# Rearranging the opening of a fused cross-attention and expert kernel: range sums, exponential table, step 0's exponentials and value banks

## The chip, the cores and the metric

The kernel runs on one core of a Trainium2 chip. The metric is the device time of one execution in microseconds (us), as the median of several runs. Engines are called PE (matmuls), PEld (its weight loads), DVE (vector), ACT (scalar), POOL (GpSimd) and SP (which issues most DMAs). PSUM, the memory that matmuls write into, has eight banks, 0 to 7, each of 128 partitions by 512 fp32.

## The reference, cut to what matters

```python
# x, ctx: [4, 256, 128]; 16 heads of 64; 64 experts, 8 taken per token
xn, ln = layer_norm(ctx), layer_norm(layernorm(x))
q = ln @ Wq
k, v = split(concatenate([xn, ln], axis=1) @ Wkv)   # 512 keys and values per batch, INNER = 1024
attn = softmax(q @ k.T * scale + mask)
x = x + layer_norm((attn @ v) @ Wout)
h = layernorm(x)
x = x + shared_expert(h) + routed_experts(h)
```

## The kernel before, in words

Every engine has its own instruction stream, written out by hand, and the engines meet through semaphores. Products that need fp32 accuracy are split in a high and a low part: a product is three matmuls (high by high, high by low, low by high: lines 761 to 763 in `three`), and every result that is used again is split by ACT (high part) and DVE (low part, which needs the high one).

The program has three stages.

**Prelude.** Weights and tokens are loaded. ACT makes the high parts of the weights (`wv_hi`, `wk_hi`, `wq_hi`), POOL the low parts. DVE computes the moments of the tokens of batches 0 and 1 (`token_moments(0)`, `spread_of(0)`, `normalise_half(0)`), then of batches 2 and 3. ACT takes the roots (`root`), normalises the context tokens (`normalise_context`), and evacuates the transposed tokens (`evac_tokens`) to `kvT`, which DVE's `split_tokens` splits in `kv_hi` and `kv_lo`. For batches 2 and 3 POOL makes `kv_lo`.

Values are kept in fp16 pairs, so they need a scale that keeps them in range. ACT sums the squares of the value weights and of the gains. One matmul with a matrix of ones (L827) spreads the two sums over all partitions, into bank 0 (`OUT_BANK`). DVE's `value_range` (L1165 to L1183) copies them out (L1169, which lifts `s_range` to 2) and computes the scale, whose last instruction lifts `s_range` to 3. It is the last thing in DVE's prelude.

**Opening.** One list, `OPENING`, gives all engines their order: 32 value chunks v0 to v31, and between them the transposes of batches 2 and 3 (t2, t3), keys and queries of the first steps (k0, q0, k1), and step 0's scores (s0, s1), biases (b0, b2) and exponentials (x0 to x3). A value chunk is three matmuls of 512 columns on PE, ACT's scaled copy (L587) and DVE's low part (L1244); its bank is free when that is done. Chunks 0 to 13 go round banks 0, 5, 3 and 4, chunks 14 to 31 round banks 0, 5 and 6. Banks 2, 3 and 4 hold scores from s0 on, bank 1 keys, bank 7 queries. An item "s" is two masked score tiles on DVE (L1202), after PE has made their scores. PE waits for `s_range` 2 before the first item, and for all 32 low parts after the last one.

**Steps.** 32 steps, each one pair of heads of one batch: scores, softmax, split, transposition, attention, projection. PE's loop starts with `clear_out()`, `keys(2)` and `queries(1)` and then `scores(1, 0)`. After the steps come the experts.

The program inserts a load of ScalarE's function table where a function isn't in the table loaded last. `Sqrt` is used in the prelude, `Exp` first in item x0.

Of the kernel before, what the change touches and what calls it, by code (L numbers as in the profile page):

```python
# [29 lines left out]
ACT = mybir.ActivationFunctionType  # L30
# [12 lines left out]
def xattn_moe(nc, x, ctx_in, mask, g_x, b_x, g_l, b_l, wq, wkv, wout, g_o, b_o,  # L43
# [13 lines left out]
    TILES = 2 * QT  # L57
# [4 lines left out]
    with stack:  # L62
        def sem(name):
            return stack.enter_context(nc.semaphore(name))
# [94 lines left out]
        ps = stack.enter_context(nc.psum_tensor("ps", [P, 8, 512], F32))  # L159
        OUT_BANK, K_BANK, SCORE_BANK, TURN_BANK, AV_BANK, Q_BANK = 0, 1, 2, 5, 6, 7  # L160
# [10 lines left out]
        def at_hi(b):  # L171
            return (b + B // 2) % B
# [18 lines left out]

        def v_bank(n):

            return (0, 5, 3, 4)[n % 4] if n < 14 else (0, 5, 6)[n % 3]

        def v_before(n):

            return max((m for m in range(n) if v_bank(m) == v_bank(n)), default=None)
# [3 lines left out]


        CHUNKS = 2 * B * KT
        between = {1: ["t2"], 3: ["t3"], 9: ["k0"], 10: ["q0"], 12: ["k1"], 14: ["s0"], 15: ["b0"], 16: ["x0", "x1"], 17: ["s1"],
                   18: ["b2"], 20: ["x2"], 22: ["x3"]}
        OPENING = [item for n in range(CHUNKS) for item in [f"v{n}"] + between.get(n, [])]
        OPENING = [(item.rstrip("0123456789"), int(item.lstrip("vtkqsxb"))) for item in OPENING]

# [11 lines left out]
        s_squares, s_range = sem("s_squares"), sem("s_range")  # L221
# [4 lines left out]
        s_table = sem("s_table")  # L226
# [12 lines left out]
        s_score, s_masked, s_exp = sem("s_score"), sem("s_masked"), sem("s_exp")  # L239
# [254 lines left out]
        def _(act):  # L494
# [4 lines left out]
            def root(half):  # L499

                act.wait_ge(s_var, half + 1)
                act.activation(rs[:, half * NT:(half + 1) * NT], tmp[:, 0, half * NT:(half + 1) * NT], ACT.Sqrt)\
                    .then_inc(s_std, 1)

            def normalise_context(b):

                if b % 2 == 0:
                    act.wait_ge(s_shift, b // 2 + 1)
                for q in range(QT):
                    j = b // 2 * NT + 4 + b % 2 * QT + q  # L510
                    ins = act.activation(tok[:, b, q, :], tok[:, b, q, :], ACT.Identity,
                                         bias=shift[:, j:j + 1], scale=rs[:, j:j + 1])
                    ins.then_inc(s_tokc, 1)

            def evac_tokens(b):

                act.wait_ge(s_kvtp, b + 1)
                for part in range(2):
                    act.activation(kvT[:, b, part * S:(part + 1) * S],
                                   ps[:, AV_BANK + b % 2, part * S:(part + 1) * S], ACT.Identity,  # L520
                                   bias=cols[:, 2 * part + 1:2 * part + 2],
                                   scale=cols[:, 2 * part:2 * part + 1]).then_inc(s_kvT, 1)
# [16 lines left out]
            evac_tokens(0)  # L539
            root(1)  # L540
            evac_tokens(1)
            normalise_context(2)
            normalise_context(3)
            act.wait_ge(s_wq, 16)
# [212 lines left out]
        def _(pe):  # L757
            def three(o, a_hi, a_lo, b_hi, b_lo, start=True, stop=True):

                skip = not (start and stop)  # L760
                pe.matmul(o, a_hi, b_hi, start=start, stop=False, skip_group_check=skip)  # L761
                pe.matmul(o, a_hi, b_lo, start=False, stop=False, skip_group_check=skip)  # L762
                return pe.matmul(o, a_lo, b_hi, start=False, stop=stop, skip_group_check=skip)  # L763
# [4 lines left out]
            def transpose_tokens(b):  # L768

                pe.wait_ge(s_tok, b + 1)  # L770
                pe.wait_ge(s_tokc, QT * (b + 1))
                if b >= 2:
                    pe.wait_ge(s_kvT, 2 * (b - 1))
                for j in range(KT):
                    mm = pe.transpose(ps[:, AV_BANK + b % 2, j * P:(j + 1) * P], tok[:, b, j, :],
                                      ident[:, :])
                mm.then_inc(s_kvtp, 1)
# [46 lines left out]
                            mm.then_inc(s_score, 1)  # L824

            pe.wait_ge(s_squares, 2)
            pe.matmul(ps[:, OUT_BANK, 0:2], ones[:, :], range_v[:, 0:2], start=True, stop=True).then_inc(s_range, 1)  # L827
            pe.wait_ge(s_wvlo, 1)
            pe.wait_ge(s_range, 2)
            for what, n in OPENING:  # L830
                if what == "v":
                    b, j, half = n // (2 * KT), n // 2 % KT, n % 2
                    if n % (2 * KT) == 0:
                        pe.wait_ge(s_kvlo, b + 1)
                    if v_before(n) is not None:
                        pe.wait_ge(s_vlo, v_before(n) + 1)
                    cut = slice(half * 512, (half + 1) * 512)
                    three(ps[:, v_bank(n), :], kv_hi[:, at_hi(b), j * P:(j + 1) * P],
                          kv_lo[:, b, j * P:(j + 1) * P], wv_hi[:, cut], wv_lo[:, cut]).then_inc(s_v, 1)
                elif what == "t":  # L840
                    transpose_tokens(n)
                elif what == "k":
                    keys(n)
                elif what == "q":
                    queries(n)
                elif what == "s":
                    if n == 0:
                        pe.wait_ge(s_klo, 1)
                        pe.wait_ge(s_qlo, 1)
                        pe.wait_ge(s_vlo, 11)  # L850
                    else:
                        pe.wait_ge(s_vlo, 12)
                    scores(0, n)
# [228 lines left out]
        def _(dve):  # L1082
            count = [0]

            def chain(ins):

                ins.then_inc(s_dve, 1)
                count[0] += 1
# [52 lines left out]
            def normalise_half(half):  # L1141
                at = half * NT
                inverse_std(NT, (s_std, half + 1), at)

                dve.scalar_tensor_tensor(out=shift[:, at + 4:at + NT], in0=mv[:, at + 4:at + NT, 0], scalar=-1.0,
                                         in1=rs[:, at + 4:at + NT], op0=ALU.mult, op1=ALU.mult)\
                   .then_inc(s_shift, 1)
                for b in (2 * half, 2 * half + 1):
                    for q in range(QT):
                        j = at + b % 2 * QT + q  # L1150
                        ins = normalise(tok[:, b, QT + q, :], x_in[:, QT * b + q, :], j)
                        if q == 0:
                            chain(ins)
                    ins.then_inc(s_tok, 1)

            def split_tokens(b):
                dve.wait_ge(s_kvT, 2 * (b + 1))
                dve.tensor_copy(kv_hi[:, at_hi(b), :], kvT[:, b, :]).then_inc(s_kvhi, 1)
                if b >= B // 2:
                    return  # L1160
                dve.wait_ge(s_kvhi, b + 1)
                dve.tensor_tensor(kv_lo[:, b, :], kvT[:, b, :], kv_hi[:, at_hi(b), :].bitcast(F32), ALU.subtract)\
                   .then_inc(s_kvlo, 1)

            def value_range():  # L1165

                bits = range_v[:, :].bitcast(I32)
                dve.wait_ge(s_range, 1)
                dve.tensor_copy(range_v[:, 2:4], ps[:, OUT_BANK, 0:2]).then_inc(s_range, 1)  # L1169
                dve.wait_ge(s_range, 2)  # L1170
                chain(dve.scalar_tensor_tensor(out=range_v[:, 4:5], in0=range_v[:, 2:3], scalar=2.0 * P,
                                               in1=range_v[:, 3:4], op0=ALU.mult, op1=ALU.mult))
                chained()
                chain(dve.tensor_scalar(bits[:, 5:6], bits[:, 4:5], 23, None, ALU.logical_shift_right))
                chained()
                chain(dve.tensor_scalar(bits[:, 5:6], bits[:, 5:6], 1, None, ALU.add))
                chained()
                chain(dve.tensor_scalar(bits[:, 5:6], bits[:, 5:6], 1, None, ALU.logical_shift_right))
                chained()
                chain(dve.tensor_scalar(bits[:, 6:7], bits[:, 5:6], -1, 205, ALU.mult, ALU.add))  # L1180
                chain(dve.tensor_scalar(bits[:, 7:8], bits[:, 5:6], 49, None, ALU.add))
                chained()
                dve.tensor_scalar(bits[:, 6:8], bits[:, 6:8], 23, None, ALU.logical_shift_left).then_inc(s_range, 1)  # L1183
# [5 lines left out]
            token_moments(1)  # L1189
            spread_of(1)  # L1190
            split_tokens(0)
            normalise_half(1)
            split_tokens(1)
            value_range()

            def mask_scores(i, t):

# [246 lines left out]
```

## Time and profile before

| what | us |
|---|---|
| median of 3 runs | 400.32 |
| lowest, highest | 398.47, 401.39 |
| the profiled execution | 398.68 |
| its span | 396.9 |
| PE busy | 350.5 (88%) |
| DVE busy | 310.2 (78%) |
| ACT busy | 288.6 (73%) |
| POOL busy | 234.5 (59%) |

The span is the time from the first to the last instruction that the profiler recorded; 1.8 us of the execution's time lie around it. The profiled execution is 1.6 us below the median of the three runs.

### The profile page before, as it was taken

Reading aid. Unit: us, or ns where it says so; the run is one execution under the profiler, and the core shown is the slowest. Engines: PE = TensorE matmul, PEld = TensorE weight load, DVE = VectorE, ACT = ScalarE, POOL = GpSimd, SP = SyncE. Lnnn points to the kernel's source line nnn. Section 1 sums busy time; section 2 is a strip of 40 time slices with the busy share of each in tenths; the row PEclk is TensorE's granted clock in tenths of the full one; section 3 lists DMA queues with packets and bytes.
Section 4 is the critical chain, followed back from the end, with each engine's and each line's share of the span. In section 5 each row is a group of like instructions: output and inputs, shape, how many; then the busy total and the mean of one; then the engine's idle time right before and its main releaser. Section 6 shows DMA issues by size and latency. Waiting matters only on the chain.

```text
span 396.9 us, 7568 instructions
## 1 busy us (share of the span) xinstructions
PE 350.5 (88%) x2381; PEld 237.9 (60%) x2381; DVE 310.2 (78%) x753; ACT 288.6 (73%) x639; POOL 234.5 (59%) x291
## 2 busy tenths in 40 slices
PE   0259797899999999999999989977899898999995
PEld 0248464566666666666666656755576675677773
DVE  2889676787877877778977877858799888888884
ACT  3469675876867768687799799956387887766662
POOL 5227220978798888887789989899188870000000
PEclk9999969999999999999999999999899999999998
DMA  7500040598979898998788986840000000000000
GB/s 243 147 1 1 2 79 0 106 176 124 183 132 176 132 177 139 168 147 155 125 175 128 158 134 114 127 80 2 2 0 1 2 1 0 2 26 1 2 0 26
DMA packets 117959, 33.65 MB, mean 85 GB/s; under 512 B 107808, under 2 KB 117536, under 8 KB 117920
## 3 DMA queue, kind: packets, MB, share of 16 engines
q1 hardware_dynamic: 117488, 31.60, 45.2%
q10 hardware_dynamic: 432, 1.57, 1.2%
q8 instruction: 19, 0.31, 0.3%
q14 instruction: 20, 0.16, 0.1%
HBM read 8.26 MB, written 0.52 MB: 22 GB/s over the span
## 4 chain that ended last, share of the span: by engine, by line
PE 62%; DVE 14%; issue 7%; ACT 7%; DMA 5%; POOL 4%; SPq 0%; DVEq 0%; ACTq 0%; POOLq 0%
PE ps L821 10%; PE ps L865 8%; PE ps L761 8%; PE ps L762 6%; PE ps L763 6%; PE ps L894 4%; PE ps L906 3%; PE ps L879 3%; PE ps L981 3%; PE ps L1001 3%; PE ps L1003 3%; PE ps L1002 3%; DMA pT<-p 2%; DMA tok<-in_ctx 2%; DVE v L1244 2%
## 5 line engine op out<-in xcount | busy, mean ns | idle before, releaser
L393 POOL TENSOR_TENSOR p<-prob,p 128x512 f16<-128x512 f32 x93 | 108.1, 1163 | 7.5
L1202 DVE CUSTOM_DVE_ANT_0 sc<-ps,mask_add 128x512 f32<-128x512 f32 x128 | 83.3, 688 | 32.9 <-PE ps L821 31.3
L555 ACT ACTIVATE prob<-sc,p_bias 128x512 f32<-128x512 f32 x128 | 91.5, 716 | 3.4 <-POOL p L393 1.4
L391 POOL CAST p<-prob 128x512 f16<-128x512 f32 x93 | 56.7, 610 | 46.7 <-ACT prob L555 33.4
L709 ACT ACTIVATE h<-ps 128x512 f32<-128x512 f32 (+1 forms) x66 | 39.3, 595 | 20.8 <-PE ps L763 20.4
L1376 DVE TENSOR_TENSOR h<-h,ps 128x512 f32<-128x512 f32 x64 | 43.8, 684 | 12.9 <-PE ps L981 12.6
L1383 DVE TENSOR_TENSOR h_lo<-h,h_hi 128x512 fp32r<-128x512 f32 (+1 forms) x66 | 49.4, 748 | 3.1 <-ACT h_hi L722 3.0
L722 ACT ACTIVATE h_hi<-h 128x512 fp32r<-128x512 f32 (+1 forms) x66 | 41.4, 627 | 14.2 <-DVE h L1376 13.5
L865 PE MATMUL ps<-pT,v 128*64 128x256 f16 x768 | 48.0, 275 | 0.0
L563 ACT ACTIVATE p_bias<-neg_max,ln_range 128x2 f32<-128x2 f32 x64 | 18.6, 290 | 37.9 <-DVE neg_max L1202 37.8
L865 PEld LDWEIGHTS ps<-pT,v 128*64 128x64 f16 x768 | 39.5, 110 | 5.2 <-issue 3.7
L761 PE MATMUL ps<-xf_hi,wu_hi 128*128 128x512 f32 x64 | 37.0, 578 | 0.0
L821 PE MATMUL ps<-k_hi,q_hi 64*128 64x512 f32 x128 | 32.0, 495 | 4.1 <-DVE neg_max L1202 2.5
L1225 DVE TENSOR_TENSOR pT<-ps,pT 128x512 f16<-128x512 f32 x35 | 23.6, 678 | 7.2 <-ACT pT L571 7.0
L1244 DVE SCALAR_TENSOR_TENSOR v<-ps,range_v,v 128x512 f16<-128x512 f32 x32 | 23.1, 749 | 7.8 <-ACT v L587 7.5
L981 PE MATMUL ps<-cwT,sel 128*128 128x512 f16 x64 | 25.2, 397 | 2.0 <-DVE h L1376 2.0
L1001 PE MATMUL ps<-h_hi,wd_hi 128*128 128x512 f32 x64 | 26.2, 409 | 0.2 <-DVE h_lo L1383 0.2
L587 ACT ACTIVATE v<-ps,range_v 128x512 f16<-128x512 f32 x32 | 21.2, 686 | 6.8 <-PE ps L763 4.0
L763 PE MATMUL ps<-xf_hi,wu_lo 128*128 128x512 f32 x64 | 25.5, 399 | 0.0
L762 PE MATMUL ps<-xf_lo,wu_hi 128*128 128x512 f32 x64 | 25.5, 399 | 0.0
L821 PE MATMUL ps<-k_lo,q_hi 64*128 64x512 f32 x128 | 25.5, 392 | 0.0
L821 PE MATMUL ps<-k_hi,q_lo 64*128 64x512 f32 x128 | 25.5, 391 | 0.0
(187 smaller groups left out, 758.9 us busy)
## 6 DMA issues: line engine op xcount, KB each, us to landing
wup_s<-in_L_ffn_W_up SPq DMA_DIRECT2D x8, 256.0 KB, 3.5
wdn_s<-in_L_ffn_W_down SPq DMA_DIRECT2D x8, 256.0 KB, 3.7
pT<-p SPq DMA_TRANSPOSE x93, 3.2
wkv_s<-in_L_xattn_Wkv ACTq DMA_DIRECT2D x2, 512.0 KB, 5.9
x_in<-in_x SPq DMA_DIRECT2D x2, 256.0 KB, 7.2
tok<-in_ctx SPq DMA_DIRECT2D x4, 128.0 KB, 8.0
wq_s<-in_L_xattn_Wq ACTq DMA_DIRECT2D x1, 512.0 KB, 8.3
wo_s<-in_L_xattn_Wout SPq DMA_DIRECT2D x1, 512.0 KB, 5.1
```

Source lines behind the costliest of these rows:

```text
L391: pool.tensor_copy(p16[:, t, 0, :], prob[:, t, :]).then_inc(s_phi, 1)
L393: pool.tensor_tensor(p16[:, t, 1, :], prob[:, t, :], p16[:, t, 0, :], ALU.subtract).then_inc(s_plo, 1)
L555: act.activation(prob[:, t, :], sc[:, t, :], ACT.Exp, bias=p_bias[:, t:t + 1], scale=-1.0, accum_out=p_sum[:, i % 2, t:t + 1]).then_inc(s_ ...
L722: act.activation(h_hi[0:rows_of(g), g % SPLIT_RING, :], h[0:rows_of(g), g % H_RING, :], ACT.Copy)\
L761: pe.matmul(o, a_hi, b_hi, start=start, stop=False, skip_group_check=skip)
L762: pe.matmul(o, a_hi, b_lo, start=False, stop=False, skip_group_check=skip)
L763: return pe.matmul(o, a_lo, b_hi, start=False, stop=stop, skip_group_check=skip)
L821: mm = pe.matmul(ps[:, score_bank(i, 2 * qt + head), :], a[rows, i // 2 % 2, at:at + P], c[rows, i % 2, :], start=(n == 0), stop=(n == 2), ...
L865: mm = pe.matmul(ps[cut, AV_BANK, 0:S], v16[:, b * KT + j, v, pair * P + head * DH:pair * P + (head + 1) * DH], pT[:, i % 2, head, p * KT ...
L1202: return dve.tensor_tensor_reduce(sc[:, t, :], ps[:, score_bank(i, t), :], mask_add[:, step(i)[2], :], -SCALE, -LEAST, ALU.add, ALU.min, n ...
L1376: dve.tensor_tensor(h[:, g % H_RING, :], h[:, g % H_RING, :], ps[:, CW_BANK + weighed(g) % 2, :], ALU.mult).then_inc(s_h, 1)
L1383: dve.tensor_tensor(h_lo[rows, g % SPLIT_RING, :], h[rows, g % H_RING, :], h_hi[rows, g % SPLIT_RING, :].bitcast(F32), ALU.subtract).then_ ...
```

## The change

- The range sums go to bank 2 (`SCORE_BANK`), and PE's wait for `s_range` 2 moves from before v0 to before s0.
- DVE's `value_range()` moves from the end of the prelude to behind `split_tokens(0)`, ahead of `normalise_half(1)`.
- ACT gets one more instruction, an `Exp` of one column, behind `evac_tokens(1)`; it brings the table load with it.
- x1 moves from directly behind x0 (chunk 16) to behind v18, and b2 from behind v18 to behind v19.
- From v20 on, chunks go round banks 5, 2, 6, 3, 0, 4. Those that use banks 2, 3 or 4 first wait until all four masked tiles of step 0 are made (`s_masked` 4).

```diff
         def v_bank(n):
-            return (0, 5, 3, 4)[n % 4] if n < 14 else (0, 5, 6)[n % 3]
+            return (0, 5, 3, 4)[n % 4] if n < 14 else (0, 5, 6)[n % 3] if n < 20 else (5, 2, 6, 3, 0, 4)[n % 6]
...
-        between = {1: ["t2"], 3: ["t3"], 9: ["k0"], 10: ["q0"], 12: ["k1"], 14: ["s0"], 15: ["b0"], 16: ["x0", "x1"], 17: ["s1"],
-                   18: ["b2"], 20: ["x2"], 22: ["x3"]}
+        between = {1: ["t2"], 3: ["t3"], 9: ["k0"], 10: ["q0"], 12: ["k1"], 14: ["s0"], 15: ["b0"], 16: ["x0"], 17: ["s1"],
+                   18: ["x1"], 19: ["b2"], 20: ["x2"], 22: ["x3"]}
...
             evac_tokens(1)
+            act.activation(tmp[:, 1, 0:1], ident[:, 0:1], ACT.Exp).then_inc(s_table, 1)
             normalise_context(2)
...
             pe.wait_ge(s_squares, 2)
-            pe.matmul(ps[:, OUT_BANK, 0:2], ones[:, :], range_v[:, 0:2], start=True, stop=True).then_inc(s_range, 1)
+            pe.matmul(ps[:, SCORE_BANK, 0:2], ones[:, :], range_v[:, 0:2], start=True, stop=True).then_inc(s_range, 1)
             pe.wait_ge(s_wvlo, 1)
-            pe.wait_ge(s_range, 2)
             for what, n in OPENING:
                 if what == "v":
...
+                    if n >= 20 and v_bank(n) in (2, 3, 4):
+                        pe.wait_ge(s_masked, TILES)
...
                     if n == 0:
+                        pe.wait_ge(s_range, 2)
                         pe.wait_ge(s_klo, 1)
...
                 dve.wait_ge(s_range, 1)
-                dve.tensor_copy(range_v[:, 2:4], ps[:, OUT_BANK, 0:2]).then_inc(s_range, 1)
+                dve.tensor_copy(range_v[:, 2:4], ps[:, SCORE_BANK, 0:2]).then_inc(s_range, 1)
...
             split_tokens(0)
+            value_range()
             normalise_half(1)
             split_tokens(1)
-            value_range()
```

## Rows read from the trace of the kernel before

**Rows 1.** Windows: stretch, length, busy PE, PEld, DVE, ACT, POOL, clock, DMA share, GB/s.

```profile
24.30:40.30 16.00, 15.98 (x62) 12.65 (x62) 14.25 (x25) 12.86 (x22) 10.15 (x5) 1.00 0.00 1
40.30:51.10 10.80, 7.15 (x31) 4.10 (x30) 7.59 (x16) 7.04 (x14) 3.47 (x4) 0.96 0.08 16
51.10:64.10 13.00, 11.46 (x33) 7.71 (x33) 9.57 (x13) 9.63 (x17) 1.77 (x2) 0.77 0.26 49
...
80.00:260.00 180.00, 177.00 (x1545) 116.43 (x1544) 143.47 (x397) 145.21 (x373) 150.86 (x183) 1.00 0.87 149
```

**Rows 2.** Timeline, prelude: start, duration, engine, line, operation [idle time before it].

```profile
13.58 2.34 POOL L370 TENSOR_TENSOR wk_lo<-wkv_s,wk_hi 128x1024 fp32r<-128x1024 f32 x1 [4.73 <-ACT wk_hi L533]
13.63 2.30 DVE L1145 SCALAR_TENSOR_TENSOR shift<-mv,rs 128x4 f32<-128x4 f32 x1
...
20.25 0.69 DVE L1162 TENSOR_TENSOR kv_lo<-kvT,kv_hi 128x512 fp32r<-128x512 f32 x1
...
21.89 0.16 DVE L1145 SCALAR_TENSOR_TENSOR shift<-mv,rs 128x4 f32<-128x4 f32 x1
...
22.09 1.65 ACT L511 ACTIVATE tok<-tok,shift,rs 128x128 f32<-128x128 f32 x4 [1.05 <-DVE shift L1145]
...
23.64 1.05 ACT L545 ACTIVATE wq_hi<-wq_s 128x1024 fp32r<-128x1024 f32 x1
...
24.32 0.77 PE L761 MATMUL ps<-wv_hi,kv_hi 128*128 128x512 f32 x1 [5.17 <-DVE range_v L1169]
...
24.77 2.37 POOL L372 TENSOR_TENSOR wq_lo<-wq_s,wq_hi 128x1024 fp32r<-128x1024 f32 x1 [8.85 <-ACT wq_hi L545]
...
25.26 1.90 DVE L1183 TENSOR_SCALAR range_v<-range_v 128x2 int32<-128x2 int32 x1
...
27.20 1.26 ACT L587 ACTIVATE v<-ps,range_v 128x512 f16<-128x512 f32 x2 [2.51 <-DVE range_v L1183]
```

**Rows 3.** Timeline of the opening, DVE alone (v4 to v9, v13 and v14).

```profile
32.49 4.04 DVE L1244 SCALAR_TENSOR_TENSOR v<-ps,range_v,v 128x512 f16<-128x512 f32 x6
...
40.52 1.43 DVE L1244 SCALAR_TENSOR_TENSOR v<-ps,range_v,v 128x512 f16<-128x512 f32 x2
```

**Rows 4.** Timeline of the opening around step 0's scores.

```profile
44.12 0.30 ACT L563 ACTIVATE p_bias<-neg_max,ln_range 128x2 f32<-128x2 f32 x1 [1.17 <-DVE neg_max L1202]
...
45.00 1.28 ACT L555 ACT_TABLE_LOAD   x1
...
46.30 0.72 ACT L555 ACTIVATE prob<-sc,p_bias 128x512 f32<-128x512 f32 x1
...
47.73 1.24 ACT L587 ACTIVATE v<-ps,range_v 128x512 f16<-128x512 f32 x2
...
49.23 0.50 PE L761 MATMUL ps<-wv_hi,kv_hi 128*128 128x512 f32 x1 [2.44 <-DVE v L1244]
...
49.70 0.69 DVE L1202 CUSTOM_DVE_ANT_0 sc<-ps,mask_add 128x512 f32<-128x512 f32 x1
...
51.11 0.79 PE L761 MATMUL ps<-wv_hi,kv_hi 128*128 128x512 f32 x1 [0.92 <-DVE v L1244]
```

**Rows 5.** Timeline, the opening's end and the first step.

```profile
61.60 0.50 PE L761 MATMUL ps<-wv_hi,kv_hi 128*128 128x512 f32 x1
...
64.13 0.39 PE L911 MATMUL ps<-zeros 128*128 128x512 f16 x1 [1.56 <-DVE v L1244]
...
65.84 0.51 PE L821 MATMUL ps<-k_hi,q_hi 64*128 64x512 f32 x2
```

**Rows 6.** Windows of the granted clock (columns as above).

```profile
50.50:51.00 0.50, 0.00 (x0) 0.00 (x0) 0.50 (x1) 0.50 (x2) 0.31 (x1) 0.50 1.13 215
...
57.00:58.00 1.00, 1.00 (x6) 0.65 (x4) 0.64 (x1) 0.77 (x2) 0.00 (x0) 1.00 0.03 5
```

**Rows 7.** Timeline where the experts start.

```profile
278.85 0.61 PE L944 MATMUL ps<-one,cw 128*128 128x128 f16 x4 [2.79 <-DVE cw L1330]
```

**Rows 8.** Window of the same place.

```profile
279.00:282.00 3.00, 3.00 (x13) 2.18 (x12) 1.58 (x3) 0.43 (x1) 0.00 (x0) 0.50 0.00 0
```

## The prediction

> **What bounds the kernel now.** I read the windows first, to see which stretches leave PE idle, and then the timelines of those. Through the attention steps PE is busy 177.0 of 180 us [rows 1]: there PE is the bound, and a step that starts earlier by some time should end earlier by the same. So the question is when step 1 starts. It starts at 64.13, when PE clears the output bank [rows 5]. Ahead of it lie three stretches. Up to 40.3 the first value chunks run with PE busy 15.98 of 16.00 us, but PE first waited 5.17 us, until DVE had copied the range sums [rows 1, 2]. From 40.3 to 51.1 PE is busy 7.15 of 10.8 us: it waits for three banks while ACT loads its table and makes x0 and x1 [rows 1, 4]. From 51.1 to 64.1 PE looks busy, but half of that is at half speed, and at the end each chunk waits for its bank [rows 1, 6]. The change works on all three.
>
> I give times below on the clock of the trace of before ("old clock"), and subtract what the prelude gives at the end.
>
> **Part 1: the start, and the scale moved forward.** Without the wait PE needs only the low part of batch 0's tokens, which ends at 20.94 (20.25 + 0.69), and not 24.15 [rows 2]. PE starts 3.3 us earlier. That is not the gain, because the next engine is late: ACT can scale v0 only behind its work on batches 2 and 3 and `wq_hi`, and that work now waits longer. DVE's range chain comes between `kv_lo` and the shift of half 1. It ran from 24.15 to 25.26 up to its last instruction; that one took 1.90 us beside POOL's `wq_lo`, while its neighbours take 0.15 [rows 2]. At 20.94 POOL is idle, so the whole chain takes 1.11 + 0.16 = 1.3 us. The shift of half 1 then ends at 22.05 + 1.3 = 23.35, ACT's four context tiles (1.65) end at 25.0, `wq_hi` at 26.0, and v0's scaling starts at 26.0 instead of 27.20. Behind it ACT has v0, v1 (1.26), the evacuation of t2 (1.0), v2, v3 (0.61 to 0.69 each), t3 (1.0) and v4 (0.69): 31.0. PE is ahead of all of them, even at half speed. So the low part of v4 starts at 31.0 instead of 32.49 [rows 3], from which on DVE has no idle time up to v14: six low parts take 4.04, 0.67 each. **Gain 1.5**, between 1.2 (ACT's own lead) and 1.7.
>
> A row of this trace bears on the order of POOL and DVE. Both DVE instructions that took 2.30 and 1.90 us started while POOL ran a two-input operation from SBUF and ended with it (15.93 against 15.92, 27.16 against 27.14), where the same L1145 takes 0.16 with POOL idle [rows 2]. The cast of batch 2's tokens is due at 28.2 now, and `wq_lo`, which moves to 26.05, ends at 28.4; I expect up to 0.3 us of waiting, and v2's low part has that much room before t3. The Trainium skill, page "SBUF — State Buffer", section "Who interferes with whom", says that a cast that takes two ports and a two-input vector instruction each exclude a GpSimd instruction on the shared ports until the first one ends. The trace agrees in both rows named.
>
> **Part 2: the table.** The load takes 1.28 us at 45.00, between v16 and x0 [rows 4]. It moves to 21.05, where ACT was idle 1.05 us and, with the shift 1.3 us later, will be idle 2.3 us [rows 2]. Load and one small `Exp` take 1.28 + 0.2 = 1.5, so they are hidden by 0.8 us. Without that cover they would cost 0.4. Scaled copies (47.73) run behind the load of before with no load of their own [rows 4], so the table of `Exp` serves the copies too, and nothing brings another load between. The Trainium skill, page "ScalarE: Activation LUTs", section "What ACT_TABLE_LOAD costs", puts a switch at 2.66 us, 1.38 of it a drain behind the load. By that the insertion would overrun its gap by some 0.5 us and the forecast would rise by as much. The row has the load at 45.00 and the exponential at 46.30, with no such drain, and I go by the row.
>
> **Part 3: from s0 on.** On the old clock v16's high part ends at 45.00 as before. Then, with durations of rows 4: x0 to 45.7, v17 to 46.4, v18 to 47.0, x1 to 47.7, v19 to 48.4. DVE makes v17's low part from 46.4 to 47.1 and the two masked tiles of s1 (0.61 to 0.69 each) to 48.4, where before the second began at 49.70 [rows 4]. PE's longest waits are now for bank 6 (v17's low part: v20 at 47.15) and for the four masked tiles (v21 at 48.5), some 0.6 us each, against 2.44 and 0.92 [rows 4]. The new wait at v21 holds v22 and everything behind it on PE, but v22 needs v18's low part, which DVE does after s1 anyway (49.1), so it costs nothing. ACT goes on without a gap: b2 (0.3) to 48.7, v20 to 49.4, x2, v21, v22, x3 and v23 (two at 0.71, three at 0.62 to 0.65) to 52.7. PE has six banks now and is not waited for. The low part of v23 starts at 52.7, and from there DVE is the slowest engine: nine low parts at 0.67 [rows 3] are 6.1 us, to 58.8. Before, a bank had to go through PE, ACT and DVE before its next matmul, with three banks; the last chunk alone, from its first matmul at 61.60 until PE goes on at 64.13, took 2.5 us [rows 5]. Step 1 starts at 58.9 instead of 64.13 [rows 5]. **Gain 5.2.** Bounds: 4.6 if every low part takes the 0.75 of a single one, 6.3 if DVE never waits for ACT from s1 on (fourteen low parts from 48.4).
>
> **Part 4: PE's clock.** What is late next is PE's own speed. With six banks PE runs ahead: v31 goes to bank 2, free after v25 at 54.7, and ends at 55.5. Then PE waits for DVE until 58.8, 3.3 us. The trace of before has two long waits: 2.44 and 0.92 us with one chunk between, after which the granted clock is 0.50 (1.2 GHz) from 50.1 to 57.0 [rows 4, 6], and 2.79 us at 276 to 278.85, after which it is 0.50 again for 3.4 us [rows 7, 8]. The wait of 1.56 at 62.6 left it at full speed [rows 5]. A wait of 3.3 lies on the side that lost it. The price: from 64.13 to 65.84 PE runs two triples, and then three pairs of score matmuls (0.7); doubled, that is 1.7 + 0.7 = **2.4 us lost**. Behind it DVE masks tiles and PE waits in any case, which hides the rest. Bounds are 0, and 3.4, half of the longest slow stretch.
>
> **The sum.** 398.68 - 1.5 - 5.2 + 2.4 = 394.4 us. The profiled execution lies 1.6 below the median; runs of this kernel spread over 2.9 us, which is what one or two slow stretches of PE come to. I forecast 394.5 and let the 1.6 widen the top of the range.
>
> **Rivals.**
> *The clock is kept.* PE's wait at the end falls so that the clock stays, or DVE is faster at the end. For it: the place of such a drop in a run depends on more than the program, as the first waits of before show (the clock was still full for the chunk at 49.23, after 2.44 us idle, and fell only around 50.1) [rows 4, 6]. Then 398.68 - 6.7 = 392.0. The Trainium skill, page "TensorE: Matmul & The Clock Gate", section "What's actually happening", says that this monitor runs free of the program, so that the same kernel changes speed at different points from run to run. One profile can't show that here.
>
> *The lead is not used.* ACT becomes the bound of the whole opening, t2 and t3 come later because `value_range` stands ahead of `normalise_half(1)`, and part 1 gives nothing; with the clock lost it comes to 395.9, and on a run 1.6 higher, as the median is, 397.5. Or the load comes back before x0: 1.28 more, 395.7. Against both: ACT's high parts take 0.62 where DVE's take 0.67, and the copy at 47.73 needs no load. These are within 1% together with the noise.
>
> *Slower.* PE loses its clock at the opening's end and doesn't regain it, because DVE-bound starts of steps leave it waiting. Attention is PE's stage, so each us at half clock costs 0.5. The change gives 6.7; to end 1% (4 us) slower than before it would have to lose 10.7, so the clock would have to stay low for 21 us. From that point on it is slower: 398.68 - 6.7 + 10.7 = 402.7. The longest stretch of before is 6.8 [rows 6], and step after step PE is full, which speaks against it.
>
> **How the numbers follow.** Clock lost 0.50 (394.5, itself 392.5 to 397), clock kept 0.34 (391 to 394), lead or load not used 0.13 (395.5 to 398), slower 0.03. About 1%, 4 us, is what a measurement of this kernel can tell from no change. Faster by more than that means under 396.3: all of the kept case, over four fifths of the lost one, a little of the third: 0.79. Within 1%: 0.18. Slower: 0.03. The range goes from 391.0 (clock kept, part 3 at its better bound) to 397.5 (clock lost, parts at their poorer bounds, and most of the 1.6).
>
> **What would show it.** The first value matmul at about 21.0, v0's scaling at 26.0, a table load at 21 and none at 43; the range chain's last instruction at 0.16 us; v23's low part at 51.2 (52.7 less 1.5) and DVE without gaps to 57.3; step 1 at 57.4 and a granted clock of 0.5 for some us behind it. The forecast fails if the low parts don't run back to back at 0.67, if ACT's queue is later than walked here at v0 or v23, or if the step's start isn't what sets the end.

## The result and the profile after

The changed kernel takes 393.37 us (median of 4 runs, 392.77 to 395.38) beside 399.7 for the kernel before in the same comparison: a ratio of 0.985, 95% interval 0.981 to 0.990. A second comparison, of the same kernel, gave 393.63 beside 397.49: 0.989, 0.985 to 0.994. The forecast was 394.5, within 391.0 to 397.5. The profiled execution took 392.77 us, span 391.0, 5.9 less than before.

In the timeline of the prelude the lines to set beside [rows 2] are these (line numbers have moved by 1 to 3):

```profile
21.09 0.15 DVE L1172 COPY range_v<-ps 128x2 f32<-128x2 f32 x1
...
21.29 1.28 ACT L542 ACT_TABLE_LOAD   x1
21.32 0.77 PE L762 MATMUL ps<-wv_hi,kv_hi 128*128 128x512 f32 x1 [1.93 <-DVE kv_lo L1165]
...
22.29 0.17 DVE L1186 TENSOR_SCALAR range_v<-range_v 128x2 int32<-128x2 int32 x1
...
23.61 1.65 ACT L511 ACTIVATE tok<-tok,shift,rs 128x128 f32<-128x128 f32 x4 [0.82 <-DVE shift L1148]
...
26.11 1.24 ACT L588 ACTIVATE v<-ps,range_v 128x512 f16<-128x512 f32 x2
26.28 2.38 POOL L372 TENSOR_TENSOR wq_lo<-wq_s,wq_hi 128x1024 fp32r<-128x1024 f32 x1 [10.13 <-ACT wq_hi L546]
...
28.29 0.66 DVE L1161 CAST kv_hi<-kvT 128x512 fp32r<-128x512 f32 x1
```

PE starts 3.0 us earlier, but ACT's scaling of v0 only 1.1 earlier (26.11 against 27.20). The scale's last instruction takes 0.17 us instead of 1.90. The table load stands in ACT's gap, with 0.82 us to spare. The cast at 28.29 starts while POOL's `wq_lo` still runs (to 28.66) and takes 0.66 us, 0.23 more than the 0.43 that such a cast takes with POOL idle. The executions start with up to 0.3 us of difference: DVE's first `kv_lo` starts at 20.25 before and at 20.49 here. Counted from it, v0 is scaled 1.3 us earlier and not 1.1.

The opening's end, again in the timeline, answers to [rows 4, 5]:

```profile
44.07 1.25 ACT L588 ACTIVATE v<-ps,range_v 128x512 f16<-128x512 f32 x2
...
45.21 0.72 ACT L556 ACTIVATE prob<-sc,p_bias 128x512 f32<-128x512 f32 x1
...
46.05 0.69 DVE L1205 CUSTOM_DVE_ANT_0 sc<-ps,mask_add 128x512 f32<-128x512 f32 x1
...
46.80 0.50 PE L762 MATMUL ps<-wv_hi,kv_hi 128*128 128x512 f32 x1 [0.24 <-DVE neg_max L1205]
...
50.82 6.02 DVE L1247 SCALAR_TENSOR_TENSOR v<-ps,range_v,v 128x512 f16<-128x512 f32 x9 [0.45 <-ACT v L588]
...
56.90 0.39 PE L914 MATMUL ps<-zeros 128*128 128x512 f16 x1 [2.31 <-DVE v L1247]
```

v17 is scaled directly behind x0, the second pair of masks ends 3.7 us earlier, PE's stalls there shrink from 2.44 and 0.92 to a few tenths, and the last nine low parts run back to back, 0.67 each. Step 1 starts at 56.90: 7.2 us earlier (7.5 counted from the first `kv_lo`). PE waits 2.31 us for it, and in this execution it keeps its clock (windows, columns as in [rows 1]):

```profile
57.00:60.00 3.00, 2.57 (x13) 1.53 (x12) 0.21 (x1) 1.20 (x2) 0.00 (x0) 1.00 0.00 0
```

So 7.2 us were won at step 1 and 5.9 are left in the span. The starts of the attention matmuls (24 per step) show where the rest went. Up to step 18 each is 7.21 to 7.25 us ahead of before. At step 20 the lead is 4.8, from step 21 on 5.4. In the changed kernel:

```profile
176.27 0.58 SPq L317 DMA_DIRECT2D go_row<-in_L_xattn_g_o  x1
...
179.19 12.67 SPq L311 DMA_TRANSPOSE pT<-p  x6
...
185.15 0.61 POOL L391 CAST p<-prob 128x512 f16<-128x512 f32 x1 [3.65 <-DMA pT<-p]
...
187.00 1.50 PE L868 MATMUL ps<-pT,v 128*64 128x256 f16 x24
187.09 0.72 ACT L556 ACTIVATE prob<-sc,p_bias 128x512 f32<-128x512 f32 x1 [0.86 <-POOL p L393]
...
188.90 0.72 ACT L556 ACTIVATE prob<-sc,p_bias 128x512 f32<-128x512 f32 x1 [0.99 <-POOL p L393]
...
191.76 0.70 PE L909 MATMUL ps<-ao,wo_s 128*128 128x256 f32 x2 [1.47 <-DVE ao L1223]
...
192.23 1.28 ACT L635 ACT_TABLE_LOAD   x1
...
195.90 1.54 PE L868 MATMUL ps<-pT,v 128*64 128x256 f16 x24
```

and in the kernel before, the same two steps:

```profile
190.81 0.61 POOL L391 CAST p<-prob 128x512 f16<-128x512 f32 x1 [3.74 <-DMA pT<-p]
...
194.81 1.50 PE L865 MATMUL ps<-pT,v 128*64 128x256 f16 x24
...
200.72 1.50 PE L865 MATMUL ps<-pT,v 128*64 128x256 f16 x24
```

Read from the top: SP issues five small loads (176.27 to 179.09) ahead of the next transpose, which goes out at 179.19 and lands 5.8 us later, where half of all transposes land within 3.2. POOL waits for it, so its parts of `prob` are late; ACT's exponentials wait for POOL, and the two table loads of the root stand behind them on ACT; PE then waits for DVE, and its clock falls:

```profile
192.60:196.00 3.40, 3.40 (x20) 1.99 (x18) 0.56 (x3) 3.33 (x7) 3.21 (x4) 0.50 1.17 221
```

Step 20 takes 8.90 us from step 19, where before it took 5.91. Two things keep this from being a plain price of the new timing. The kernel before has the same wait of POOL (3.74), and its step 19 took 7.17 us against 6.61 here. What differs is the place: POOL's cast behind the wait starts 4.75 us after the attention of step 18 here, 3.16 before. And PE is busy through all 3.40 us at half clock, so the clock alone may be worth up to 1.7 of the 3.0 us (an estimate: half of 3.40).

### The profile page after: what moved, and what is told of

Its sections match the earlier page's. It is cut to its first block, busy times and chain, and to the rows that moved or that the text cites. A ratio compares the mean times of both kernels' runs of the same rounds, so it can differ in the third digit from the quotient of the medians.

```text
span 391.0 us, 7575 instructions
## 1 busy us (share of the span) xinstructions
PE 348.0 (89%) x2381; PEld 236.1 (60%) x2381; DVE 306.2 (78%) x753; ACT 287.1 (73%) x640; POOL 233.7 (60%) x291
## 3 DMA queue, kind: packets, MB, share of 16 engines
q10 hardware_dynamic: 432, 1.57, 1.3%
## 4 chain that ended last, share of the span: by engine, by line
PE 51%; DVE 13%; DMA 10%; ACT 8%; issue 8%; POOL 8%; SPq 0%; DVEq 0%; ACTq 0%; POOLq 0%
PE ps L822 8%; DMA pT<-p 7%; PE ps L868 7%; PE ps L762 6%; PE ps L764 5%; PE ps L763 5%; POOL p L393 4%; POOL p L391 3%; PE ps L984 3%; PE ps L1004 3%; PE ps L1006 3%; PE ps L1005 3%; PE ps L897 3%; PE ps L909 3%; PE ps L882 3%
## 5 line engine op out<-in xcount | busy, mean ns | idle before, releaser
L909 PE MATMUL ps<-ao,wo_s 128*128 128x256 f32 x64 | 22.2, 428 | 4.4 <-DVE ao L1223 4.4
L1234 DVE TENSOR_TENSOR k_lo<-ps,k_hi 128x512 fp32r<-128x512 f32 x32 | 22.0, 686 | 4.9 <-ACT k_hi L577 4.8
```

## The experiments

Two theories stood against each other in most of them: that the opening is one queue after another (ACT up to v23, DVE behind it), so that each part of the change gives its own amount; and that one or two parts do it all. I read each profile where PE clears the output bank (step 1, "clear") and where the attention of step 0 starts. Differences to the changed kernel are taken from its first profile as they stand; where it matters, the difference counted from the first `kv_lo` (20.49 there) follows in square brackets.

**The changed kernel again.**

> The changed kernel once more, unchanged. Step 1 started at 56.90 in its first profile, 7.2 us ahead of before, but the span ended only 5.9 us ahead: 1.8 us went between steps 16 and 20. If that loss is a chance of this one execution (transfers that took longer), this profile shows step 1 at 56.9 and step 20 still 7.2 ahead, a span near 389.5. If it follows from the new timing (the expert loads now fall differently among the transposes), it loses 1.5 to 2 us at the same steps again, span 391.

Clear 56.72, as in the first profile. But the wait of 2.32 us cost PE its clock this time:

```profile
56.72 0.61 PE L914 MATMUL ps<-zeros 128*128 128x512 f16 x1 [2.32 <-DVE v L1247]
...
60.99 0.69 DVE L1205 CUSTOM_DVE_ANT_0 sc<-ps,mask_add 128x512 f32<-128x512 f32 x1 [4.33 <-PE ps L822]
```

```profile
56.70:59.80 3.10, 3.08 (x7) 1.98 (x7) 0.00 (x0) 0.60 (x1) 0.00 (x0) 0.50 0.00 0
59.80:62.00 2.20, 1.24 (x9) 0.74 (x10) 1.01 (x3) 0.60 (x1) 0.00 (x0) 1.00 0.00 0
```

From clear to the attention of step 0 it took 11.60 us here and 10.25 in the first profile. That is the price of the clock at this place: 1.35 (1.34 to 1.44 in all the profiles that pay it). Of all profiles with the changed kernel's opening (five, with three of the runs further down), three lost the clock there (11.60, 11.59, 11.69) and two kept it (10.25, 10.25), with 2.31 or 2.32 us of waiting in each. Two of the runs below belong beside them: the scale computed last waited 2.28 us there and kept the clock (10.22 to the attention of step 0), x1 back waited 2.84 and lost it (11.66). From step 16 to step 22 this profile took 40.04 us, the first 41.16, before 39.35: the loss came again, smaller. Neither forecast holds as it stood; the later runs take it up.

**The scale computed last.**

```diff
             split_tokens(0)
-            value_range()
             normalise_half(1)
             split_tokens(1)
+            value_range()
```

> The changed kernel with the scale's computation put back at the end of DVE's prelude; PE still starts without waiting for it. My theory: PE's start isn't the bound, ACT's scaling of v0 is, and the chain's last instruction stands behind POOL's wq_lo again. v0 scaled at about 27.2 (26.1 after), step 1 at 58.0 to 58.3, 1.1 to 1.4 us later. Rival: the 1.90 us of that instruction were not due to POOL; then it takes 0.16, the scale is ready at 25.5, v0 is scaled at 25.5 or as soon as wq_hi is done, and step 1 comes 0.5 us earlier than in the changed kernel.

```profile
25.21 2.37 POOL L372 TENSOR_TENSOR wq_lo<-wq_s,wq_hi 128x1024 fp32r<-128x1024 f32 x1 [9.20 <-ACT wq_hi L546]
25.36 2.25 DVE L1186 TENSOR_SCALAR range_v<-range_v 128x2 int32<-128x2 int32 x1
27.64 0.69 ACT L588 ACTIVATE v<-ps,range_v 128x512 f16<-128x512 f32 x1 [2.51 <-DVE range_v L1186]
```

The instruction starts 0.15 us after POOL's and ends with it (27.61 and 27.58). ACT, free since 25.13, waits 2.51 us for it. v0 is scaled 1.53 later, and clear is at 58.66, 1.76 later [1.9], more than the 1.1 to 1.4 of my forecast, since the instruction took 2.25 us and not 1.90. PE also ran at half speed from 29.6 to 33.0 in this execution; what that adds isn't measured apart. The rival is out.

**The table loaded in front of x0.**

```diff
-            act.activation(tmp[:, 1, 0:1], ident[:, 0:1], ACT.Exp).then_inc(s_table, 1)
```

> The changed kernel without the early exponential: the table is loaded in front of x0 again. My theory: ACT's queue is on the path from v16 to v23, so all of the load, 1.3 us, comes back at step 1 (58.2). Rival: with six banks and the exponentials spread DVE is the bound behind s0, and the load is hidden in part: step 1 within 0.5 us of 56.9.

Clear 58.90, 2.0 later [2.25], more than the load.

```profile
43.22 1.28 ACT L555 ACT_TABLE_LOAD   x1
...
45.93 0.75 DVE L1246 SCALAR_TENSOR_TENSOR v<-ps,range_v,v 128x512 f16<-128x512 f32 x1 [1.95 <-ACT v L587]
...
46.74 0.50 PE L761 MATMUL ps<-wv_hi,kv_hi 128*128 128x512 f32 x1 [1.74 <-DVE v L1246]
...
48.79 0.63 PE L761 MATMUL ps<-wv_hi,kv_hi 128*128 128x512 f32 x1
...
50.31 0.69 ACT L587 ACTIVATE v<-ps,range_v 128x512 f16<-128x512 f32 x1 [0.23 <-PE ps L763]
```

The load comes through to the masks in full, and PE, after a wait of 1.74, falls to half speed (a matmul of 0.63 at 48.79), so that from 50.3 to 52.3 ACT and DVE wait for PE. My theory holds and left out this second price. The rival is out.

**Three banks from v14 on.**

```diff
-            return (0, 5, 3, 4)[n % 4] if n < 14 else (0, 5, 6)[n % 3] if n < 20 else (5, 2, 6, 3, 0, 4)[n % 6]
+            return (0, 5, 3, 4)[n % 4] if n < 14 else (0, 5, 6)[n % 3]
```

> The changed kernel with banks 0, 5 and 6 alone from v14 on. My theory: chunks from v20 on take 0.92 each (bank round trip over three banks) instead of 0.67, eleven of them, and step 1 comes 2 to 2.8 us later, at 59 to 59.7. Rival: the banks mattered only while ACT was stalled by its table load, so step 1 is at most 0.7 us later.

```profile
54.52 0.50 PE L762 MATMUL ps<-wv_hi,kv_hi 128*128 128x512 f32 x1 [0.15 <-DVE v L1247]
...
55.52 2.09 ACT L588 ACTIVATE v<-ps,range_v 128x512 f16<-128x512 f32 x3 [0.43 <-PE ps L764]
56.24 2.16 DVE L1247 SCALAR_TENSOR_TENSOR v<-ps,range_v,v 128x512 f16<-128x512 f32 x3 [0.37 <-ACT v L588]
58.46 0.39 PE L914 MATMUL ps<-zeros 128*128 128x512 f16 x1 [1.57 <-DVE v L1247]
```

Clear 58.46, 1.56 later [1.5]: between the two forecasts, nearer to mine. Chunks go in threes of 2.52 us (DVE at 53.72, 56.24), 0.84 each where six banks give 0.67. I had taken 0.92.

**x1 back behind x0, b2 behind v18.**

```diff
-                   16: ["x0"], 17: ["s1"], 18: ["x1"], 19: ["b2"],
+                   16: ["x0", "x1"], 17: ["s1"], 18: ["b2"],
```

> The changed kernel with x1 directly behind x0 and b2 behind v18 again. My theory: v17's high part comes one exponential (0.71) later, so DVE's second pair of masked tiles and everything behind it does too: step 1 0.7 us later, at 57.6. Rival: ACT does the same work before v23 in either order and is never idle, so step 1 stays at 56.9 within 0.2.

```profile
46.71 0.69 DVE L1205 CUSTOM_DVE_ANT_0 sc<-ps,mask_add 128x512 f32<-128x512 f32 x1
...
47.44 0.29 ACT L564 ACTIVATE p_bias<-neg_max,ln_range 128x2 f32<-128x2 f32 x1 [1.46 <-DVE neg_max L1205]
```

Clear 58.13, 1.23 later [1.3] where I had 0.7. The masks come 0.66 later, as I had it, and ACT now waits 1.46 us in front of b2 (0.18 in the changed kernel) with v19 still behind it: 0.66 and one copy of 0.62 make the 1.28 by which v23 is late. The rival's "never idle" is wrong.

**What the four make of the whole time.** In one comparison, beside 397.49 of before, the changed kernel took 393.63, with the scale last 394.02, with the late table 392.90, with three banks 393.38; x1 back took 393.62 beside 397.88. The ratios are 0.989, 0.990, 0.989, 0.988 and 0.990, each with 0.003 to 0.005 on either side, 1.3 to 2.1 us. So what each part gives at step 1 (1.2 to 2.0 us) is shown by the timelines and can't be told in the medians. One reason is in the profiles: the late table and three banks leave PE a last wait of 1.57 us, and it keeps its clock, where the changed kernel waits 2.31 and pays 1.35 in three profiles of five. How much of the medians that explains isn't shown.

**Only PE's wait moved**, on the kernel before (the sums in bank 2, as in the change).

```diff
             pe.wait_ge(s_wvlo, 1)
-            pe.wait_ge(s_range, 2)
...
                     if n == 0:
+                        pe.wait_ge(s_range, 2)
```

> The kernel before with the range sums in a bank of their own and PE's wait for them moved to s0, nothing else. My theory: PE starts 3.2 us earlier and nothing comes of it, since ACT can't scale v0 before 27.2: step 1 at 63.8 to 64.4 (64.13 before). Rival: PE's late start held the opening, and step 1 comes 1.5 to 3.2 us earlier.

PE starts at 21.34, 3.0 us earlier. Counted from the first `kv_lo`, v0 is scaled at the same time as before (6.94 and 6.95 us behind it), and step 1, at 63.93 against 64.13, comes 0.45 earlier. Median 398.22 beside 397.88, ratio 1.000 (0.998 to 1.003). This is the clearest run of all: the engine that had shown the wait of 5.17 us in the profile wasn't late. In the changed kernel this part may not even be needed: there DVE has copied the sums by 21.24, and PE starts at 21.32 in any case, behind `kv_lo`. By these rows the old wait would cost about 0.1 us (an estimate; no run put it back).

**Only the six banks**, on the kernel before: its `v_bank` and the wait that goes with it as in the change.

```diff
-            return (0, 5, 3, 4)[n % 4] if n < 14 else (0, 5, 6)[n % 3]
+            return (0, 5, 3, 4)[n % 4] if n < 14 else (0, 5, 6)[n % 3] if n < 20 else (5, 2, 6, 3, 0, 4)[n % 6]
...
+                    if n >= 20 and v_bank(n) in (2, 3, 4):
+                        pe.wait_ge(s_masked, TILES)
```

> The kernel before with six value banks from v20 on, nothing else. My theory: the stall at the table load stays, but from v23 on DVE's low parts follow one another at 0.67 instead of 0.92 to 1.28: step 1 at 61.4, 2.7 us ahead of before. Rival: the stall at v20 costs PE its clock whatever the banks, and step 1 gains at most 1 us.

Clear 61.79, 2.34 earlier than before, near my 2.7: the nine low parts run back to back from 55.71. The rival, at most 1 us, is out; PE's slow stretch is 3.4 us long here (50.5 to 53.9) and 6.8 in the kernel before. Median 395.26, ratio 0.995 (0.993 to 0.998).

**Step 1 begun early**, to see what PE's wait and DVE's 2.95 us behind it are worth.

```diff
-            pe.wait_ge(s_vlo, CHUNKS)
-            pe.wait_ge(s_woscaled, 1)
-            clear_out()
             keys(2)
             queries(1)
+            pe.wait_ge(s_vlo, CHUNKS - 2)
+            pe.wait_ge(s_woscaled, 1)
+            clear_out()
...
                     scores(i, 0)
+                if i == 1:
+                    pe.wait_ge(s_vlo, CHUNKS)
```

> The changed kernel with PE's first work of step 1 taken out of the wait for all low parts: keys(2) and queries(1) run directly behind v31, the output bank is cleared and scores(1, 0) made as soon as v29's low part is done, and the wait for all 32 stands in front of step 0's later work. PE's 2.3 us of waiting are filled and DVE's masks of step 1 follow v31's low part without the 2.9 us of waiting seen after. If that waiting is on the path, DVE's first mask of step 1 moves from 59.8 to 57 and the kernel ends 2 to 2.8 us earlier than the changed one. If DVE's waiting is hidden by what the steps need otherwise, under 0.5 us.

```profile
51.45 5.35 DVE L1248 SCALAR_TENSOR_TENSOR v<-ps,range_v,v 128x512 f16<-128x512 f32 x8
...
55.29 0.60 ACT L577 ACTIVATE k_hi<-ps 128x512 fp32r<-128x512 f32 x1
...
56.09 0.50 PE L822 MATMUL ps<-k_hi,q_hi 64*128 64x512 f32 x2
...
57.27 0.69 DVE L1206 CUSTOM_DVE_ANT_0 sc<-ps,mask_add 128x512 f32<-128x512 f32 x1 [0.47 <-PE ps L822]
```

Keys and scores of step 1 are made while DVE still works on the last chunks; its first mask is at 57.27 instead of 59.79. The attention of step 0 starts at 64.65, 2.5 ahead of the changed kernel where it keeps its clock and 3.7 where it doesn't. PE's longest wait left there is 1.06 us, and the granted clock stays full. Median 388.23 beside 397.88, ratio 0.977 (0.975 to 0.980). The changed kernel's ratios were 0.985 and 0.989, so this is 0.8 to 1.2% (3 to 5 us) below it, at or above the 2 to 2.8 forecast. Of this 2.5 is seen at the mask. The clock's price in the runs that pay it, and the loss at steps 16 to 22 (39.4 us here against 40.0 and 41.2), would account for the rest; that isn't measured apart.

**Where the loss at steps 16 to 22 comes from.** Between these steps the program loads expert weights (those of steps 17 and 20, 512 KB each), five small tensors (step 18), and ACT's table twice. First the expert loads were put at steps 2 to 9:

```diff
-                if i % 3 == 2 and i // 3 < PAIRS:
+                if 2 <= i < 2 + PAIRS:
...
-                    load_experts(i // 3)
+                    load_experts(i - 2)
```

> The changed kernel with the eight pairs of expert loads issued at steps 2 to 9 instead of every third step from 2 to 23. From the attention of step 16 to that of step 22 the profiles so far took 38.6 to 41.7 us (41.2 and 40.0 in the two of the changed kernel), all other stretches repeat to 0.1 us in most. Theory: the transposes behind an expert load at steps 14 and 17 land late by a varying amount, POOL then waits for the transposes and the steps run out of their lead; without loads there this stretch takes under 39 us and the kernel ends 1 to 1.5 us earlier. Rival: the five small loads at step 18 or the table loads at steps 19 and 20 make that loss; then the stretch stays at 39.5 to 41.

Then the small loads alone were put at step 22:

```diff
-                if i == FIRST + 2:
+                if i == FIRST + 6:
                     load_late()
```

> The changed kernel with the five small loads moved from step 18 to step 22. If they make the loss between steps 16 and 22, the stretch takes under 39 us; if the expert loads do, it stays at 39.5 to 41. The small loads are needed at step 24, so nothing else should move.

and both together:

> Both moves together. If transfers among the transposes are the whole of it, the stretch from step 16 to step 22 comes to 38.3 or less, and its spread from run to run goes. If it stays at 39 or more, ACT's two table loads at steps 22 and their work (2.6 us) are what is left.

Time between starts of the attention matmuls, us:

| kernel | steps 0 to 10 | 10 to 16 | 16 to 22 | 22 to 31 | longest wait of POOL for a transpose, steps 16 to 22 | median, ratio to before |
|---|---|---|---|---|---|---|
| before | 62.64 | 37.56 | 39.35 | 57.33 | 3.74 | |
| changed, first profile | 62.60 | 37.56 | 41.16 | 57.41 | 3.65 | 393.37, 0.985 |
| changed, again | 62.63 | 37.56 | 40.04 | 57.64 | 4.09 | 393.63, 0.989 |
| scale last | 62.60 | 37.56 | 38.95 | 57.12 | 2.24 | 394.02, 0.990 |
| late table | 62.64 | 38.46 | 41.72 | 57.28 | 4.06 | 392.90, 0.989 |
| three banks | 62.61 | 37.56 | 39.83 | 58.61 | 3.86 | 393.38, 0.988 |
| x1 back | 62.64 | 37.56 | 38.63 | 57.32 | 2.35 | 393.62, 0.990 |
| wait only | 62.64 | 37.56 | 39.51 | 57.12 | 3.87 | 398.22, 1.000 |
| six banks only | 62.62 | 37.56 | 39.65 | 57.24 | 3.87 | 395.26, 0.995 |
| step 1 early | 62.60 | 37.56 | 39.43 | 57.41 | 4.13 | 388.23, 0.977 |
| expert loads early | 63.97 | 38.55 | 38.72 | 56.67 | 2.11 | 393.52, 0.990 |
| small loads late | 62.64 | 37.56 | 38.63 | 58.57 | 0.83 | 391.44, 0.984 |
| both | 64.64 | 37.56 | 38.80 | 57.86 | 0.90 | 393.20, 0.991 |
| step 1 early, expert loads early | 62.64 | 37.69 | 38.65 | 56.68 | 2.05 | 388.21, 0.977 |

The last four kernels have loads moved, the ten above them don't. Three things can be read from the table. The long wait of POOL comes with the small loads: it stands at the same step in all twelve kernels that issue them at step 18 (2.05 to 4.13), and no wait is over 0.90 in the two that don't. How long it is depends on how late the first transpose behind them lands: after 5.2 to 5.8 us in eight profiles, which gives waits of 3.65 to 4.13, and after 3.8 or 3.9 in the two with the scale last and x1 back; with the expert loads early it is 3.4 both times, which gives 2.05 and 2.11. And the stretch is at 38.6 to 38.95 wherever that wait is 2.35 or less and at 39.35 to 41.72 wherever it is 3.65 or more.

So both kinds of load have a part in it, and moving either one brought the stretch to 38.6 to 38.8. But x1 back got 38.63 with no load moved: ten profiles without a move spread from 38.63 to 41.72, and four with one can't settle how much is chance. Nor is the loss peculiar to the change, since the kernel before is among the ten.

Whether the loss moves elsewhere isn't shown either. With the expert loads at steps 2 to 9 the first ten steps take 1.3 and 2.0 us more in two profiles of three, and steps 10 to 16 take 1.0 more in one, but so they do with the late table, where no load was moved. With the small loads at step 22 the last stretch takes 1.2 more (step 25 took 9.19 us where it is 7.4 before, with the root's table loads, at 225.47 and 226.98, inside it and PE at half speed from 227.5), but with three banks it is as long. Of the forecasts, that of a gain of 1 to 1.5 us in the whole time failed, and so did 38.3 or less with both moves (38.80). The medians of these three kernels don't stand apart from the changed kernel's; the intervals are 0.003 to 0.005 wide on each side.

**Step 1 early and the expert loads at steps 2 to 9** (last line of the table):

> The kernel that begins step 1 early (388.2 us beside 397.9 of before) with the expert loads at steps 2 to 9. By the theory of late transposes it ends another 0.5 to 1 us earlier, near 387.5; by the rival there is no difference, or a loss, since the loads at steps 2 to 9 now stand in front of more transposes in a row.

Median 388.21 (386.07 to 390.40) beside 397.04, ratio 0.977 (0.972 to 0.981). The profiled span was 385.7, the shortest here. The median isn't better than with step 1 early alone (388.23), so the move of the loads is worth nothing that these runs can tell. The best kernel of this study is the one with step 1 begun early.

## Why the prediction was right, step by step

**What bounds the opening, and that PE's start isn't it.** Right. v0's scaling was forecast at 26.0 and came at 26.11; with the wait alone moved nothing was won (63.93 against 64.13).

**Part 1, gain 1.5.** Right in mechanism: v16's high part ends 1.5 us earlier than before (43.47 against 45.00), and with the scale computed last, step 1 comes 1.76 us later. One length was misread: the range chain takes 1.20 us up to its last instruction (24.06 to 25.26), not 1.11. The clash with POOL was shown both ways: 0.17 us beside an idle POOL, 2.25 beside a busy one. The waiting of up to 0.3 us that I put on the cast of batch 2 was 0.23.

**Part 2, the table.** Hidden by 0.82 us, as forecast (0.8). Taken back it costs 2.0 [2.25], of which 1.28 are the load; behind it PE runs at half speed, which I hadn't counted and which fits the rest. The Trainium skill's figure for a switch ("ScalarE: Activation LUTs", "What ACT_TABLE_LOAD costs": 2.66 us) isn't what these rows show: the load is 1.28 and the next instruction follows at once (43.22 + 1.28, exponential at 44.51).

**Part 3, gain 5.2.** Nearly right: v23's low part at 50.82 (51.2 forecast), nine at 0.67 to 56.84 (57.3 forecast). With part 1 the forecast for step 1 was 57.4 and it came at 56.90, so 7.2 instead of 6.7. The parts don't add up to it by themselves: taken out one by one they cost 1.76, 2.0, 1.56 and 1.23, in sum 6.55 (7.0 of 7.5 counted from the first `kv_lo`). Where the rest belongs, no run shows.

**Part 4, the clock, 2.4 lost.** The step that was off, in size and in place. PE's wait was forecast at 3.3 and is 2.31: v31 ended at 54.6 instead of 54.0 and DVE was done 0.5 earlier. At this length the clock was lost in three of five profiles, so neither "lost" nor "kept" was the one answer; I had given 0.50 and 0.34. The page that I had named for this (the Trainium skill, "TensorE: Matmul & The Clock Gate", "What's actually happening": the point of change differs from run to run of one kernel) agrees with these five profiles, 2.31 or 2.32 us of waiting in each. The price is 1.34 to 1.44, not 2.4: I had doubled all of PE's work up to the second half of step 1, while part of it is done during waits that are there in any case (0.97 in front of the second pair of scores at full speed).

**The sum.** Half right by luck. "A step that starts earlier by some time should end earlier by the same" held to 0.04 us up to step 18 and then failed: 1.8 us went at steps 19 to 21, behind a transpose that landed late and with PE at half speed from 192.6 to 196.0. The prediction had neither. So the first profile kept the clock where I had given it up and paid for it at another place. The kernel again lost 0.7 over steps 16 to 22, step 1 early 0.1: this loss isn't a fixed part of the change. The median, 393.37 and 393.63, lies between the two cases that I had put at 392.0 and 394.5.

**The spread of the runs.** I put it down to slow stretches of PE. That is wrong in the main: the four first runs of the changed kernel have mean granted clocks of 0.991, 0.993, 0.994 and 0.998 and took 392.77, 395.38, 393.25 and 393.48. The clock has some part in it: over 17, 16 and 19 runs of the kernel before in the later comparisons, the time falls as the mean clock rises (correlations -0.42, -0.68, -0.24). The profiles show another source, transposes that land late by a different amount each time.

**The rivals.** That the lead isn't used is refuted by the same rows, up to step 18. That the clock stays low is refuted: each slow stretch of the granted clock in these profiles, but for the last few us, lasted 3.4 us, except one of 6.8 in the kernel before and in the one with only PE's wait moved.

## What to carry to other kernels

The engine with the longest wait in the profile need not be the one to free: follow its result to the next engine that needs it and ask when that one could have started. Before an opening is cut short, look at the hand-over behind it: a wait for "everything done" in front of the next stage may stand in front of work that needs none of it, and taking that apart was worth more per line here than any part of the change. And before a difference of one or two us in a single profile is put down to an edit, look at the same stretch in profiles where the edit isn't: steps 16 to 22 spread over 3.1 us here with every load in its place.

## What the runs showed of the hardware that I had not expected

- The same wait of PE (2.31 or 2.32 us, with full work before and behind it) left the granted clock at 1.00 in two profiles and went with a fall to 0.50 in three, so a single profile doesn't tell whether such a wait costs the clock. A wait of 1.74 us with one chunk and another short wait behind it lost it too (table in front of x0).
- How much a tiny DVE instruction can cost beside POOL: a shift of two elements per partition took 2.25 us when it started 0.15 us behind POOL's 2.37 us subtraction and ended with it, and 0.17 us with POOL idle.
- What five small loads (32 to 64 KB) can cost: issuing them takes SP 2.8 to 3.1 us, the transpose behind them lands after 3.4 to 5.8 us (3.2 is the median of all), and POOL waits 2.05 to 4.13 us for it at this step in twelve profiles, at most 0.90 in the two without them there.
